# Window attention and two depthwise convolutions: the residual x added by an accumulating transfer to a projection that ScalarE writes out; taps of the last convolution on 127 columns

## What is computed

```python
x = layernorm2d(x0, ln_w, ln_b)                     # over channels
q, k = split(conv1x1(x, qk_w, qk_b)); vs = conv1x1(x, vs_w, vs_b)
local = depthwise3x3(vs, depth_w) + depth_b
v1, v2 = vs[:, :48], vs[:, 48:]
# q, k, v1 rolled by -4; softmax attention in 8x8 windows, 4 heads of 12; rolled back: y
y = concat([y, v2])
s = (y + local).mean(over the image)
ca = sigmoid(fu2 @ leaky_relu(fu1 @ s))
y = y * ca + local * (1 - ca)
z = conv1x1(y, proj_w, proj_b) + x0
```

## Time and profile before

| | |
|---|---|
| median of three runs | 1500.32 us |
| profiled execution: time, span | 1503.79 us, 1502.2 us |
| TensorE matmuls, weight loads | 1323.6 us (88%), 782.0 us (52%) |
| VectorE | 1263.8 us (84%) |
| ScalarE | 875.8 us (58%) |
| GpSimd | 230.8 us (15%) |
| DMA | 203.07 MB, 135 GB/s, all of the kernel's transfers on SP's queue |
| granted TensorE clock | 0.984 of full speed |

### The profile page before, as it was taken

One profiled execution on the slowest core, in us unless ns is written; L12 is line 12 of the kernel. 1 busy time (PEld: TensorE's weight loads), 2 busy tenths in 40 slices (PEclk: granted clock), 3 DMA queues, 4 the chain that ended last, 5 costly groups with the idle time before them and its releaser, 6 DMA issues.

```text
span 1502.2 us, 38208 instructions
## 1 busy us (share of the span) xinstructions
PE 1323.6 (88%) x12403; PEld 782.0 (52%) x12403; DVE 1263.8 (84%) x2222; ACT 875.8 (58%) x2279; POOL 230.8 (15%) x741
## 2 busy tenths in 40 slices
PE   5989898889899999989899999988989998888986
PEld 3666666555555555555555555555555555433332
DVE  3565656479999999999999999999989998999998
ACT  2566666666666666776566666765666666622221
POOL 2111111111122211221111211220112011000000
PEclk9999999999999999999999999999999999999999
DMA  2121212345665566645655566646655664678884
GB/s 62 51 82 55 81 55 81 99 98 148 167 148 144 138 152 165 156 114 154 166 147 139 138 159 156 156 114 159 155 125 141 161 155 112 164 181 195 211 199 126
DMA packets 81357, 203.07 MB, mean 135 GB/s; under 512 B 15248, under 2 KB 19112, under 8 KB 81320
## 3 DMA queue, kind: packets, MB, share of 16 engines
q1 hardware_dynamic: 81320, 202.60, 53.9%
HBM read 136.57 MB, written 64.91 MB: 134 GB/s over the span
## 4 chain that ended last, share of the span: by engine, by line
PE 36%; ACT 20%; DVE 16%; issue 13%; DMA 13%; ACTq 1%; DVEq 0%; SPq 0%; POOL 0%; POOLq 0%
DMA qd<-nmx 12%; PE banks_s L521 9%; ACT pt L811 5%; PE banks_t L529 5%; PE banks_t L483 5%; ACT km L767 4%; DVE mx L1009 4%; ACT ybuf L799 4%; PE banks_g L612 4%; PE banks_g L496 4%; DVE mixed L1181 3%; PE banks_g L614 3%; DVE oo L1192 3%; ACT vw L780 2%; DVE zs L1204 2%
## 5 line engine op out<-in xcount | busy, mean ns | idle before, releaser
L1181 DVE SCALAR_TENSOR_TENSOR mixed<-vin,c_pack,mixed 96x1024 f32<-96x1024 f32 x352 | 450.0, 1278 | 6.6
L1192 DVE SCALAR_TENSOR_TENSOR oo<-zs,l_w,oo 96x1024 f32<-96x1024 f32 x192 | 245.1, 1276 | 8.3 <-ACT oo L847 4.1
L811 ACT ACTIVATE pt<-banks_t 128x512 f32<-128x512 f32 x256 | 138.6, 593 | 129.0 <-PE banks_t L529 127.5
L1009 DVE TENSOR_REDUCE mx<-banks_s 128x8 f32<-128x512 f32 x260 | 167.6, 687 | 48.1 <-PE banks_s L521 47.3
L529 PE MATMUL banks_t<-qd,km 64*128 64x128 f32 x2048 | 152.8, 290 | 30.1 <-DMA qd<-nmx 30.0
L521 PE MATMUL banks_s<-km,qd 64*128 64x128 f32 x2080 | 152.9, 286 | 18.9 <-issue 15.2
L980 DVE BATCH_NORM_STATS2 bn<-banks_a 128x6 f32<-128x96 f32 x528 | 99.0, 249 | 80.5 <-PE banks_a L471 80.1
L521 PEld LDWEIGHTS banks_s<-km,qd 64*128 64x128 f32 x2080 | 129.7, 189 | 70.7 <-DVE mx L1009 40.4
L612 PE MATMUL banks_g<-vin,proj_t 128*96 128x512 f32 (+1 forms) x288 | 150.2, 622 | 11.4 <-DMA ycat<-y_img 5.7
L529 PEld LDWEIGHTS banks_t<-qd,km 64*128 64x128 f32 x2048 | 127.9, 192 | 49.9 <-issue 26.1
L434 POOL COPY vrow<-vw 96x16 f32<-96x16 f32 (+2 forms) x520 | 153.4, 349 | 0.0
(11 more groups left out here) (148 smaller groups left out, 1842.5 us busy)
## 6 DMA issues: line engine op xcount, KB each, us to landing
vin<-v_img SPq DMA_DIRECT2D x64, 495.0 KB, 5.9
v_img<-vrow SPq DMA_DIRECT2D x130, 198.0 KB, 2.8
xc<-in_x SPq DMA_DIRECT2D x134, 192.0 KB, 2.6
x<-in_x SPq DMA_DIRECT2D x64, 384.0 KB, 7.2
out<-oo SPq DMA_DIRECT2D x64, 384.0 KB, 3.0
y_img<-ybuf SPq DMA_DIRECT2D x128, 99.0 KB, 2.0
ycat<-v_img SPq DMA_DIRECT2D x64, 198.0 KB, 4.9
ycat<-y_img SPq DMA_DIRECT2D x64, 198.0 KB, 7.0
```

The source lines that it names most:

```text
L811: fn(pt[:, 2 * r + n, :], banks_t[:, n, :], ACT.Exp).then_inc(pt_done, 1)
L1009: v.tensor_reduce(mx[:, n, :, 4 * r:4 * r + 4].rearrange("q h e -> q e h"), banks_s[:, n, :].rearrange("q (e h k) -> q e h k", h=2, k=K), ...
L1181: v.scalar_tensor_tensor(out=mb[:C, par, :, 0:W], in0=vin[:C, par, 1 + dh:1 + dh + WS, 1 + dw:1 + dw + W], scalar=depth_w[:, DVE_TAPS[m]:D ...
L1192: v.scalar_tensor_tensor(out=oo[:, par, :, :], in0=zs[:, at:at + WS, 1 + dw:1 + dw + W], scalar=l1_w[:, n:n + 1], in1=oo[:, par, :, :], op ...
```

## The change

- x is no longer loaded into a tile of its own. `finish` on VectorE is gone. ScalarE writes z + z_bias into `zs` (`z_out`, L871 of the changed kernel) at the start of its strip, ahead of `exps(t, 0)`, and sets `zs_done`. GpSimd waits for that (`add_x`, L449), does a small operation on the new tile `rest`, and issues a transfer from x in DRAM that adds to `zs` (`accum_op=ALU.add`), which sets `x_added`. `tap0` waits for `x_added`. SP has neither the load of x nor the wait for `zs_done` ahead of it.
- `add_x` stands ahead of `to_image` and `wrap` in GpSimd's strip, and GpSimd's program now runs through the tail as well.
- `zs` is 2 x 9 x 128: each strip has its own halo row, and there are no zero columns. The halo is copied in every strip. ScalarE does the tap straight above (index 1), VectorE the taps 0, 2 and 3, each on the 127 columns for which it has an input.

```diff
+            def add_x(u, par):
+                s = pool.snap(u) if not isinstance(u, int) else u
+                b, j = (s // NS, s % NS) if isinstance(s, int) else (pool.snap(s // NS), pool.snap(s % NS))
+                pool.wait_ge(add_turn, FREE + u)
+                pool.wait_ge(zs_done, u + 1)
+                nc.gpsimd.tensor_tensor(rest[:], rest[:], rest[:], ALU.add).then_inc(add_turn, 1)
+                pool.dma_start(zs[:, par, 1:1 + WS, :], x[b, :, bass.ds(j * WS, WS), :],
+                               accum_op=ALU.add).then_inc(x_added[par], 16)
...
+            def z_out(u, par, late=False, after=None):
+                act.wait_ge(z_done, u + 1)
+                if not (isinstance(u, int) and u < 2):
+                    act.wait_ge(l1_step, NL * (u - 1))
+                if after is not None:
+                    act.wait_ge(mid_dve, N_MID * after + Z_BIAS)
+                of = banks_t if late and par == 1 else banks_g
+                fn(zs[:, par, 1:1 + WS, :].rearrange("c r x -> c (r x)"), of[:C, :, :].rearrange("c a n -> c (a n)"),
+                   ACT.Identity, bias=z_bias[:]).then_inc(zs_done, 1)
...
-            def tap0(u, um, par):
-                act.wait_ge(zs_done, u + 1)
-                if par == 0:
-                    act.wait_ge(halo_done, um + 1)
+            def tap0(u, um, par, after=None):
+                act.wait_ge(x_added[par], 16 * (um + 1))
+                act.wait_ge(halo_done, u + 1)
                 act.wait_ge(stored[par], FREE + 16 * um)
...
-                fn(oo[:, par, :, :], zs[:, at:at + WS, 1 + dw:1 + dw + W], ACT.Identity,
-                   scale=l1_w[:, 0:1], bias=l1_b[:]).then_inc(tap_done, 1)
...
+                fn(oo[:, par, :, :], zs[:, par, 1 + dh:1 + dh + WS, :], ACT.Identity,
+                   scale=l1_w[:, L1_FIRST:L1_FIRST + 1], bias=l1_b[:]).then_inc(tap_done, 1)
...
+                if prev:
+                    z_out(u - 1, k, late, after)
                 if attend:
                     exps(t, 0)
...
-                dh, dw = L1_TAPS[n]
-                at = par * WS + 1 + dh
-                v.scalar_tensor_tensor(out=oo[:, par, :, :], in0=zs[:, at:at + WS, 1 + dw:1 + dw + W],
-                                       scalar=l1_w[:, n:n + 1], in1=oo[:, par, :, :],
+                tap = L1_REST[n - 1]
+                dh, dw = L1_TAPS[tap]
+                to, of = slice(max(0, -dw), W - max(0, dw)), slice(max(0, dw), W + min(0, dw))
+                v.scalar_tensor_tensor(out=oo[:, par, :, to], in0=zs[:, par, 1 + dh:1 + dh + WS, of],
+                                       scalar=l1_w[:, tap:tap + 1], in1=oo[:, par, :, to],
                                        op0=ALU.mult, op1=ALU.add).then_inc(l1_step, 1)
-
-            def finish(u, um, par, late=False):
-                dve.wait_ge(z_done, u + 1)
-                dve.wait_ge(x0_loaded[par], 16 * (um + 1))
-                dve.wait_ge(tap_done, FREE + u)
...
-                v.scalar_tensor_tensor(out=zs[:, 1 + par * WS:1 + (par + 1) * WS, 1:1 + W], in0=z, scalar=z_bias[:],
-                                       in1=x0[:, par, :, :], op0=ALU.add, op1=ALU.add).then_inc(zs_done, 1)
...
-                if prev:
-                    sp.wait_ge(zs_done, before)
-                sp.dma_start(x0[:, par, :, :], x[b, :, bass.ds(top, WS), :]).then_inc(x0_loaded[par], 16)
```

More of the change, by code:

```diff
@@ L77 @@
 L1_TAPS = TAPS[:4]
-NL = len(L1_TAPS) - 1
+L1_FIRST = 1
+L1_REST = (0, 2, 3)
+NL = len(L1_REST)
 LAG = NS + 1
 GATED = 15
+Z_BIAS = 17
 N_POOL = 9
@@ L245, in program @@
         W_LOADS = 3
-        N_ZERO = 11
+        N_ZERO = 12
         N_PAD = N_ZERO + 8
@@ L452, in _ @@
             wrap(2)
[L453 to L459, removed]
+            strip(0, 1, prev=False)
+            with pool.Fori(1, NS // 2 + 1) as h:
+                for k in range(2):
+                    strip(h, k, prev=False)
+            with pool.Fori(NS // 2 + 1, B * NS // 2) as h:
+                for k in range(2):
+                    strip(h, k)
+            with pool.Fori(B * NS // 2, B * NS // 2 + NS // 2 + 1) as h:
+                for k in range(2):
+                    strip(h, k, attend=False)
         @block.tensor
@@ L904, in projections, with strip @@
                 fn(proj_m[C:128, :], projT[of[2], :], ACT.Copy, scale=free[2]).then_inc(proj_done, 1)
-            def strip(h, k, attend=True, y=True, ahead=False, prev=False, gate=None, gated=None):
+            def strip(h, k, attend=True, y=True, ahead=False, prev=False, gate=None, gated=None, late=False, after=None):
                 t = 2 * h + k
                 u = t - LAG
+                if prev:
+                    z_out(u - 1, k, late, after)
                 if attend:
@@ L924, in strip @@
                 if prev:
-                    tap0(u - 1, h - NS // 2 - 1, k)
-                    if k == 1 and gated is None:
-                        halo(u)
+                    tap0(u - 1, h - NS // 2 - 1, k, after)
+                    if gated is None:
+                        halo(u, 1 - k)
                 if attend:
@@ L949, in _ @@
             strip(NS // 2, 1, ahead=True, gated=0)
-            with act.Fori(NS // 2 + 1, NS) as h:
+            strip(NS // 2 + 1, 0, ahead=True, prev=True, after=0)
+            strip(NS // 2 + 1, 1, ahead=True, prev=True)
+            with act.Fori(NS // 2 + 2, NS) as h:
                 for k in range(2):
@@ L956, in _ @@
                 strip(h0, 1, ahead=True, prev=True, gated=b - 1)
-                with act.Fori(1, NS // 2) as hh:
+                strip(h0 + 1, 0, ahead=True, prev=True, after=b - 1)
+                strip(h0 + 1, 1, ahead=True, prev=True)
+                with act.Fori(2, NS // 2) as hh:
                     for k in range(2):
@@ L962, in _ @@
             strip(h0, 1, attend=False, y=False, ahead=True, prev=True, gated=B - 1)
-            with act.Fori(h0 + 1, h0 + NS // 2) as h:
+            strip(h0 + 1, 0, attend=False, y=False, ahead=True, prev=True, late=True, after=B - 1)
+            strip(h0 + 1, 1, attend=False, y=False, ahead=True, prev=True, late=True)
+            with act.Fori(h0 + 2, h0 + NS // 2) as h:
                 for k in range(2):
-                    strip(h, k, attend=False, y=False, ahead=True, prev=True)
-            strip(h0 + NS // 2, 0, attend=False, y=False, prev=True)
+                    strip(h, k, attend=False, y=False, ahead=True, prev=True, late=True)
+            strip(h0 + NS // 2, 0, attend=False, y=False, prev=True, late=True)
+            z_out(B * NS - 1, 1, late=True)
             tap0(B * NS - 1, B * NS // 2 - 1, 1)
@@ L1228, in last @@
                 u, um, par = 2 * h + k - LAG, h - NS // 2 - 1 + k, 1 - k
-                for m in range(NT - 1):
+                for m in range(NT):
                     mix(u, par, m, True)
-                finish(u - 1, h - NS // 2 - 1, k, late=True)
-                mix(u, par, NT - 1, True)
                 for n in range(1, NL + 1):
@@ L1319, in _ @@
             last(h0 + NS // 2, 0)
-            finish(B * NS - 1, B * NS // 2 - 1, 1, late=True)
             for n in range(1, NL + 1):
```

39 lines of the change are left out of this document (22 added, 17 removed).

## The result

The changed kernel took 1512.13 us (median of 4 runs, 1510.97 to 1513.51) beside 1500.32 for the kernel before: ratio 1.0075, 95% interval 1.0058 to 1.0093. It is slower, by 0.75%; 1487 and faster was predicted. The time lies inside the range, on the side given 0.31.

The account below looks back on a forecast made before the run. It took the mixed stage to be bound by the wait chain through the move of the maxima, the tail by VectorE. Terms -22 -3.5 -2.5 +10 +5 gave -13 us off the 1500.3 median: 1487 us, range 1468 to 1520.

Parts of the forecast that it names:

- the side given 0.31: Whole kernel: the chance given to the change making it slower, beside 0.57 for faster and 0.12 for the same.
- x leaves SP's queue: Mixed stage: the move of the maxima lands sooner, ending TensorE's 26.1 us of waits for it; -22 us.
- finish leaves VectorE: Gated strips: TensorE no longer waits for finish, -3.5 us; change to the tail: three fewer finishes, -2.5 us.
- POOL adds x: GpSimd's small operation and issue take 1.2 us together; its other work and SP's loads stay where they are.
- D: Time from POOL's issue of the adding transfer to its landing; about 5 us taken in mixed strips, 5.8 in the tail.
- Wait at tap0 in mixed strips: Mixed strips: tap0's wait for x_added costs nothing with a landing up to 8.3 us after issue; 0 us.
- The tail: Convolution alone: a three-strip round through the addition's landing lengthens the period from 10.4 to 11.1 us; +10 us.
- The end: After the last project_mixed: z_out, POOL and a landing of about 4 us replace finish; +5 us.
- 127 columns: Taps on eight fewer elements, under 10 ns each, and the halo copied every strip: nothing.
- the quick addition: Rival, chance 0.12: in the tail the addition lands as quickly as a store, about 3 us; 1472 us.
- The change of stage: Mixed stage to tail: VectorE does three finishes of 1.28 us less, some turning into waits; -2.5 us.
- the addition is slow in the tail: Rival, chance 0.27: tap0 waits for x_added in the three-strip round; a landing of 9 us gives 1507 us.

Follow-up runs that it names:

- Experiment 1: The kernel before, with x still loaded by SP but issued behind the move of the maxima, finish still on VectorE: 1478.86 us, ratio 0.9843.
- Experiments 10 and 11: At the change to the tail, ScalarE's image sums before tap0 and z_out before the scalings: on the changed kernel 1507.52 us; with old-style x load and finish from strip 48, 1467.59.
- experiment 3: The changed kernel with GpSimd's transfer as a plain copy of x over zs, addition left out: 1503.28 us, ratio 0.9999.
- experiments 7 to 9: Changed kernel: only 4 of 8 rows added, 1499.41 us; only 1 row added, 1488.55; whole addition, but SP's tail loads bring one row for eight, 1481.84.
- Experiments 8 and 9: Changed kernel: only 1 of 8 rows (48 KB) added, 1488.55 us; whole addition, but SP's tail loads bring one row for eight, 1481.84.
- experiment 2: The changed kernel, but from strip 48 on SP loads x and VectorE does finish as before: 1476.75 us, ratio 0.982.

## Why the prediction was wrong

It said -13 us, and the profiled executions differ by +7: 20 us missed. The medians are 25 off, because the profiled execution of the kernel before lay 3.5 us above its median and that of the changed one 1.2 below.

1. *x leaves SP's queue*, and 2. *finish leaves VectorE* in mixed strips: right in mechanism, small in size. -25.5 predicted, -37.0 measured. Experiment 1 has 24 for the queue, against my 22. For the other I counted only the 3.5 us of gated strips; once the wait for the move is gone, waits of TensorE for finish appear (8.9 us in experiment 1), and z_out takes those away as well.
3. *POOL adds x*: 1.2 us allowed, 1.1 us from z_out's end to the start of the issue, with the 0.8 us of the issue inside D; nothing delayed. Right.
4. *Wait at tap0 in mixed strips*: 0, right; D was 4.8 us, 5 was assumed.
5. *The tail*: **the term that failed**. +10 predicted, +27.4 measured, and 4.8 more for the first strip, whose addition landed after 9.7 us. Two things were wrong in it. D was taken from SP's own load of x in the kernel before, 5.8 us; the median was 8.0, and the landings on the chain took 8.0 to 9.1. And the round was written over three strips, (27.5 + D)/3, because I followed SP and TensorE and left out ScalarE's order: with z_out on ScalarE, behind `first`, D stands in a round of two strips, and in a second one nearly as long. With D = 5.8 the three-strip form gives 11.1 and the two-strip forms 11.0 and 10.2, so at the assumed D the wrong round did no harm. With the 8.0 of the median the three-strip form gives 11.8 and the first two-strip form 12.1, with the chain's mean of 8.7 the latter gives 12.4; 12.31 was measured. How the 17 us missed divide between D and the round depends on the D that is put in, since the landings alternate. With the median 14 x (11.8 - 11.1) = 10 are D. With the mean of the tail, 6.8 us, the three-strip form gives 11.4, and D is a smaller part: then it is the round over two strips, which meets the long landing each time, that costs most. At the tail's start the lower clock of TensorE has a part as well (5.43 us for six matmuls that took 2.82 in the earlier trace rows).
6. *The end*: +5 predicted, +4.6 measured. Right.
7. *127 columns*: 1.268 us a tap for 1.276. Nothing, as said.

Two slips in its sums change nothing: z_out enters the tail's round as 1.26 us and the other terms as 1.16 (1.10 was measured), and the quick addition's sum is 1473, not 1472.

The change of stage was the second miss: -2.5 predicted, +8.2 measured. I counted three finishes of VectorE and did not ask what stands behind ScalarE's new waits. Behind tap0, which now waits for a landing, stood the image sums; z_out stood behind the scalings. Experiments 10 and 11 get 7 and 9 us back by reordering them.

The rival that came true is "the addition is slow in the tail". Its break-even of D = 7.8 rested on a gain of 28 us; with the 37 of the mixed stage D = 8.0 alone would not have made the kernel slower: by my round, 20 for the periods, 5 at the end and 5 for the first landing leave a gain of 7. The change of stage (8 lost) and the round over two strips (7) used that up and more. The argument that I wrote into that rival, that the addition reads what it writes, is the smaller part (experiment 3). Its other one, a stretch in which DMA is 80% busy, is the larger (experiments 7 to 9), though the mean share does not tell it: in the changed kernel it is 0.64 in the mixed stage, where D is 4.8, and 0.68 in the tail. What counts is whether SP issues its loads within about a microsecond of the addition, and I should have drawn from it that no landing read from the old arrangement carries over. By the Trainium skill, "DMA: Bandwidth & Descriptors", section on the anatomy of one DMA on the gpsimd path, the estimate for a plain copy was 2.9 us; 3.7 was measured for one in the mixed stage. Its section "Issuing engines are not separate DMA queues" says that transfers of all engines interleave on the same DMA engines. Experiments 8 and 9 agree: 48 KB took 2.3 to 2.5 us in the tail when issued well ahead of the loads and 6.6 to 7.6 among them, and smaller loads brought the long landings of the whole addition from 8.7 to 6.2.

## What to carry to other kernels

When work moves to another engine, write down that engine's order first and look for the rounds that its new waits close, in every stage, the change of stage included: an in-order wait for a transfer delays all that stands behind it. Price a landing by what will be in flight beside it, not by its bytes alone, look at single landings before trusting a median (here two kinds alternate, and the chain meets only the long one), and keep an addition by DMA to stages that have slack for it; here the same edit gains 37 us in one stage and loses 45 in the next, and a version that uses it in the first only beats both kernels. Where two rounds are nearly equal, an edit to one shows little: change what they share.

## What the runs showed of the hardware

- An adding transfer of 384 KB into SBUF landed in 4.8 us in the mixed stage, a plain one in 3.7, both from GpSimd; adding 192 and 48 KB took 3.6 and 2.5. In the tail the same transfers landed in about these times when SP's loads were issued 1.3 us or more after them, and 4 to 5 us later when the loads were issued within about a microsecond of them. GpSimd spends 0.8 us on an adding issue and 0.5 on a plain one.
- SP's own issue of a load took 1.8 to 2.2 us in six of thirteen strips of the changed kernel's tail, where the addition was in flight, here from SP's timeline (start, us); the same issue took 0.4 to 0.5 us in the kernel before and with the tail of experiment 2. With a plain copy (experiment 3) the longest were 0.7 to 1.3 us, with half of the addition 1.1 to 1.4, with one row 0.5 to 0.7. No experiment was aimed at its cause.

```profile
1323.22 0.32 SPq L315 DMA_DIRECT2D vin<-v_img  x1
1323.73 2.18 SPq L316 DMA_DIRECT2D ycat<-v_img  x1
1326.09 0.32 SPq L318 DMA_DIRECT2D vin<-v_img  x1
```

- A small move queued behind a 384 KB load of the same queue cost TensorE 0.5 to 0.7 us a strip; issuing it ahead of the load, and nothing else, made this kernel 1.6% faster.
